# One bank of PSUM for every use, and new lists for four engines, in a vision transformer block on one core

## The chip, the core and the metric

One core of a Trainium2 chip runs the whole program. Its engines are TensorE (PE), VectorE (DVE), ScalarE (ACT), GpSimd (POOL) and SyncE (SP, which issues the DMAs). The metric is the device time of one execution in microseconds, the median of several runs.

## What is computed

For each of 128 images: 196 patches of 16x16 in three colours go through the real part of a 2-D FFT, weights and a projection to 192 features; a class token and positions are added (197 tokens). Then attention with 12 heads of 16 features, and after it attention with 12 heads of 64 features, whose queries and keys are layer-normalised per head and whose heads are weighted by gates (two shared, the best 2 of 10 routed).

```python
h = _L0_tok_ref(x, ...)                       # FFT patches, projection, class token, positions
h = h + _L0_attn_ref(_layernorm(h), ...)      # softmax(q k / 4) v, 12 heads of 16, then Wo
h = h + _L0_ffn_ref(_layernorm(h), ...)       # q, k normalised per head; softmax(q k) v; gates; proj
```

## The kernel before

The weights are loaded and prepared once. Then the images run through a software pipeline: the kernel works on four images at once, each at another stage. The order is written out by hand, in `ORDER`: one list of steps for PE, DVE, ACT and POOL. An entry such as `3:qk1_0` says: step `qk1`, number 0, of image i + 3. Each engine runs its list once a pass (`run_phases`), 131 passes for i from -3 to 127; steps whose image doesn't exist are left out at both ends. The engines share only semaphores: a step waits for what its data need, and for room in its PSUM bank.

PSUM has 8 banks of 128 x 512 numbers. Each use of a bank is one step's result on PE: it waits until the bank's last reader is done (`room_for`), signals that it is full (`made`), and the last reader signals it free (`read_out`). The banks are given out in `bank_uses` from `BANKS`: each kind of step has a ring, taken in the order of PE's list. `qk1` and `s1` share banks 0 and 1; `tok`, `x1T`, `v1`, `ctx` and `wo` have bank 2; `rstd`, `s2`, `pT`, `o2` and `proj` share 3, 4 and 5; `x2T`, `gl`, `qk` and `v2` have bank 6 and `ms` bank 7.

The steps, by image, with lines of PE and of who reads the bank:

- `fold` (DVE, L895) adds two mirrored halves of the image; `tok` (PE) projects it; DVE adds positions (L901) and takes the moments; POOL takes the root (L454); `nx1` normalises on DVE (L886 to L890).
- `x1T` turns it (L538), copied by ACT (L722) and DVE (L911). `qk1_0` to `qk1_2` make queries and keys of four heads each in fp16 halves: two copies on ACT (L731, L732), the low part on DVE (L916). `v1` goes to ACT (L737).
- `s1_0`, `s1_2` ... `s1_10`: scores of two heads at a time, on two banks, in 32-row parts of the array. DVE takes the negated maximum (L921), ACT the exponential with its sum (L745, twice a head), which frees the bank. DVE divides into v (`ctx`, L929, L933), `ctx0` to `ctx2` on PE in 32-column parts, copied by ACT (L751); `wo` follows, added by DVE (L943) with the second moments.
- `nx2`, `x2T` (L726, L953), `gl` and `gate` (DVE, ACT L763), `qk0` to `qk5` (copied by ACT, L756), squares on POOL (L493), `ms0` to `ms2` sum them in 32-column parts, `var` (ACT L770 to L775, DVE L1003 to L1007) takes the root. `rstd0` to `rstd5` spread it (PE), applied by DVE (L1028); high parts on ACT (L780 `rstd`, L785 `kh`), low parts on DVE (L1012 `lo`, L1018 `kl`).
- `s2_0` ... `s2_10`: scores of two heads, 64-row parts; maximum on DVE (L1034), exponential on ACT (L792); `gr` on DVE (L1041, L1044) and `sc` on POOL (L489) weight them; `pT_0` to `pT_11` turn them (L684), copied by ACT (L798); `o2_0` to `o2_5` in 64-column parts (ACT L803); `v2_0` to `v2_3` (DVE L996); `proj` (DVE L1051), then the store.

All matmuls but the turns of `pT` and `x1T`, `x2T` have line L500, that of a helper. `lasts` picks, of several steps, the last on each bank, so that one wait a bank is made.

Of the kernel before, what the change touches and what calls it, by code (L numbers as in the profile page):

```python
# [176 lines left out]
def bank_uses():  # L177

    uses, in_bank, turn = {}, [[] for _ in range(8)], {}
    for ahead, name, n in steps_of("pe"):  # L180
# [966 lines left out]
```

## Time and profile before

| | |
|---|---|
| Time, median of 3 runs | 6208.34 us (6207.62 to 6211.28) |
| The profiled execution | 6208.79 us, span 6207.0 us |
| PE busy | 5808.5 us, 94% |
| DVE busy | 5098.7 us, 82% |
| ACT busy | 4936.7 us, 80% |
| POOL busy | 2435.5 us, 39% |
| DMA | 17 GB/s over the span |

Busy time counts an engine while at least one instruction is in it; the ends of matmuls are modelled. The page cuts the span in 40 equal slices; the windows and the timeline show any stretch, in us from the span's start. In the timeline like instructions in a row are merged to one row.

### The profile page before, as it was taken

How to read it: one execution, taken by the hardware profiler on the slowest of the kernel's cores; microseconds unless marked ns; L12 is line 12 of the kernel's file. 1: busy time of each engine (PE TensorE's matmuls, PEld its weight loads, DVE VectorE, ACT ScalarE, POOL GpSimd, SP SyncE). 2: the span in 40 equal slices, each digit the busy share in tenths (PEclk: the TensorE clock that was granted, in tenths of full speed). 3: DMA queues.
4: the chain of work that ended last, by engine and by line, in shares of the span. 5: the costliest groups of instructions: out<-in, count | busy, mean ns of one | idle time of the engine just before them, and what ended most of it. 6: DMA issues, size and time to landing. Idle time of an engine off the chain costs nothing.

```text
span 6207.0 us, 204792 instructions
## 1 busy us (share of the span) xinstructions
PE 5808.5 (94%) x63792; PEld 4640.1 (75%) x63792; DVE 5098.7 (82%) x16573; ACT 4936.7 (80%) x18945; POOL 2435.5 (39%) x2438
## 2 busy tenths in 40 slices
PE   3899999999999999999999999999999999999998
PEld 3677777777777777777777777777777777777776
DVE  4788888888888888888888888888888888888886
ACT  1788887887888888788888878888887887888886
POOL 0333443343344344334334433433433343444343
PEclk8999999999999999999999999999999999999999
DMA  1000000000000000000000000000000000000000
GB/s 64 16 19 16 15 19 16 15 15 19 16 15 19 16 15 15 19 16 15 19 16 15 17 17 16 15 19 16 15 19 16 15 15 19 16 15 19 16 15 5
DMA packets 60493, 106.58 MB, mean 17 GB/s; under 512 B 8077, under 2 KB 33945, under 8 KB 60129
## 3 DMA queue, kind: packets, MB, share of 16 engines
q1 hardware_dynamic: 60456, 106.12, 5.6%
q8 instruction: 21, 0.34, 0.0%
q14 instruction: 16, 0.12, 0.0%
HBM read 86.72 MB, written 19.37 MB: 17 GB/s over the span
## 4 chain that ended last, share of the span: by engine, by line
PE 60%; DVE 27%; issue 8%; ACT 4%; DVEq 1%; SPq 0%; ACTq 0%; POOL 0%; DMA 0%; POOLq 0%
PE bank L500 54%; PE bank L684 6%; DVE nmax L1034 5%; DVE qkn L1028 4%; DVE qk L916 3%; ACT p L745 3%; DVE kl L1018 2%; DVE ql L1012 2%; DVE v L996 2%; DVE nmax L921 2%; DVE gn L1044 1%; DVE x1T L911 1%; DVE rsum L1041 1%; DVE rsum L929 0%; DVE glog L963 0%
## 5 line engine op out<-in xcount | busy, mean ns | idle before, releaser
L489 POOL TENSOR_TENSOR pq<-pq,gn 99x788 f32<-99x788 f32 x768 | 1166.3, 1519 | 2302.6 <-DVE gn L1044 2302.4
L792 ACT ACTIVATE pq<-bank,nmax 99x197 f32<-99x197 f32 x3072 | 1303.1, 444 | 300.5 <-DVE nmax L1034 300.5
L745 ACT ACTIVATE p<-bank,nmax 99x197 f32<-99x197 f32 x3072 | 1281.9, 441 | 31.2 <-DVE nmax L921 15.1
L921 DVE TENSOR_REDUCE nmax<-bank 99x2 f32<-99x394 f32 x1536 | 824.4, 565 | 320.8 <-PE bank L500 316.8
L1034 DVE TENSOR_REDUCE nmax<-bank 99x2 f32<-99x394 f32 x1536 | 837.9, 559 | 125.3 <-PE bank L500 110.1
L798 ACT ACTIVATE pT<-bank 99x394 f32<-99x394 f32 x1536 | 773.1, 512 | 152.7 <-PE bank L684 152.3
L684 PE MATMUL bank<-ident,pq 99*99 99x99 f32 (+1 forms) x6144 | 784.7, 260 | 14.8 <-ACT pq L792 3.3
L500 PE MATMUL bank<-x2T,wqkc 128*128 128x198 f16 (+1 forms) x7680 | 796.3, 249 | 1.0 <-ACT qkc L756 0.6
L684 PEld LDWEIGHTS bank<-ident,pq 99*99 99x99 f32 (+1 forms) x6144 | 647.5, 166 | 171.1 <-issue 78.4
L500 PEld LDWEIGHTS bank<-x2T,wqkc 128*128 128x128 f16 (+1 forms) x7680 | 650.0, 98 | 99.1 <-ACT qkc L756 41.4
L792 ACT ACTIVATION_READ_ACCUMULATOR pq<-bank,nmax 99x1 f32 x3072 | 687.9, 224 | 0.0
L745 ACT ACTIVATION_READ_ACCUMULATOR p<-bank,nmax 99x1 f32 x3072 | 677.0, 220 | 0.0
L493 POOL TENSOR_TENSOR sq<-qkc 128x396 f32<-128x396 f32 x768 | 660.2, 866 | 31.4 <-ACT qkc L756 24.7
L500 PE MATMUL bank<-pT,v 128*64 128x197 f32 x6144 | 633.7, 341 | 0.2 <-ACT pq L792 0.2
L780 ACT ACTIVATE qh<-qkn,ln_b 128x198 f16<-128x198 f32 x768 | 361.2, 470 | 334.2 <-DVE qkn L1028 334.1
L1028 DVE SCALAR_TENSOR_TENSOR qkn<-bank,ln_w,qkc 128x198 f32<-128x198 f32 x1536 | 575.7, 416 | 10.5 <-PE bank L500 5.0
L500 PE MATMUL bank<-qk 32*99 32x197 f16 x6144 | 418.8, 254 | 173.0 <-DVE qk L916 127.3
L500 PE MATMUL bank<-wp,oT 128*99 128x192 f32 x3072 | 530.6, 329 | 0.5 <-ACT oT L803 0.5
L500 PE MATMUL bank<-wv,x2T 128*99 128x384 f16 (+1 forms) x2560 | 518.2, 333 | 1.4 <-DVE v L996 1.4
L500 PEld LDWEIGHTS bank<-qk 32*99 32x99 f16 x6144 | 264.7, 120 | 336.6 <-issue 122.7
L500 PEld LDWEIGHTS bank<-wp,oT 128*99 128x99 f32 x3072 | 489.7, 166 | 18.3 <-ACT oT L803 1.1
L500 PEld LDWEIGHTS bank<-pT,v 128*64 128x64 f32 x6144 | 391.7, 137 | 129.6 <-issue 42.4
(149 smaller groups left out, 11877.8 us busy)
## 6 DMA issues: line engine op xcount, KB each, us to landing
xa<-in_xa SPq DMA_DIRECT2D x128, 300.1 KB
xb<-in_xb SPq DMA_DIRECT2D x128, 300.1 KB
out_tokens<-res SPq DMA_DIRECT2D x128, 74.2 KB
out_tokens<-res SPq DMA_DIRECT2D x128, 73.5 KB
p<-in_wq SPq DMA_DIRECT2D x1, 1152.0 KB
pT<-in_wk SPq DMA_DIRECT2D x1, 1152.0 KB
qkc<-in_basis SPq DMA_DIRECT2D x1, 661.5 KB
sq<-in_wq SPq DMA_DIRECT2D x1, 576.0 KB
```

The source lines that it names most:

```text
L489: nc.gpsimd.tensor_tensor(pair, pair, factor, op=ALU.mult).then_inc(s_sc.up(), 1)
L493: nc.gpsimd.tensor_tensor(sq[:, t], qkc[:, t], qkc[:, t], op=ALU.mult).then_inc(s_sq.up(), 1)
L500: return nc.tensor.matmul(o, l, r, start=first, stop=last)
L684: last = nc.tensor.transpose(o[0:TC, k * T + c * TC:k * T + c * TC + n], pq[0:n, h % SLOTS, c, k * TC:k * TC + TC], ident[0:n, 0:n])
L745: last = nc.scalar.activation(p1[0:TC, h, c, :], psum("s1", h)[0:TC, c * T:c * T + T], ACT.Exp, bias=nmax1[:, c, h:h + 1], accum_out=sum1[ ...
L780: nc.scalar.activation(qh[:, t, :], qkn[:, t % QKN_SLOTS, 0, :], ACT.Identity, bias=ln_b[:, 0:1]).then_inc(s_hi.up(), 1)
L792: last = nc.scalar.activation(pq[0:TC, h % SLOTS, c, 0:T], psum("s2", h)[0:TC, c * T:c * T + T], ACT.Exp, bias=nmax2[:, h, c:c + 1], accum ...
L798: nc.scalar.activation(pT[0:TC, h].rearrange("p a b -> p (a b)"), psum("pT", h)[0:TC, 0:2 * T], ACT.Copy).then_inc(free("pT", h), 1)
L916: V.scalar_tensor_tensor(qk1[:, g, 1].rearrange("p a b -> p (a b)"), psum("qk1", g)[:, 0:2 * TP], E1 ** -0.25 / W_SCALE, qk1[:, g, 0].rear ...
L921: V.tensor_reduce(nmax1[:, :, h], psum("s1", h)[0:TC, 0:2 * T].rearrange("p (a b) -> p a b", a=2), op=ALU.max, axis=AX.X, negate=True).the ...
L1028: last = V.scalar_tensor_tensor(qkn[:, t % QKN_SLOTS, s, :], psum("rstd", t)[:, s * TP:s * TP + TP], ln_w[:, s:s + 1], qkc[:, t, s, :], AL ...
L1034: V.tensor_reduce(nmax2[:, h, :], psum("s2", h)[0:TC, 0:2 * T].rearrange("p (a b) -> p a b", a=2), op=ALU.max, axis=AX.X, negate=True).the ...
```

## The change

The rings are gone. In PE's list each entry names its bank after an @, two digits where a step has two results: `3:s1_0@51` puts head 0 in bank 5 and head 1 in bank 1. The lists of all four engines are ordered anew. `LEAD` = 2 writes out two passes more at each end of the loop as straight code, and the count that a wait is for is worked out in another form for it. `lasts` is gone: a step that needs several banks read waits for the last of them. `ms` is numbered 0 in place of 2. The edits that repeat the ones below (o2, gr and DVE's ctx as PE's ctx; var as ms) are left out.

```diff
@@ -127,33 +127,30 @@
 
 
 
-BANKS = {"tok": (2,), "x1T": (2,), "qk1": (0, 1), "v1": (2,), "s1": (0, 1), "ctx": (2,), "wo": (2,),
-         "x2T": (6,), "gl": (6,), "qk": (6,), "v2": (6,), "ms": (7,),
-         "rstd": (3, 4, 5), "s2": (3, 4, 5), "pT": (3, 4, 5), "o2": (3, 4, 5), "proj": (3, 4, 5)}
-
 ORDER = {
     "pe": """
-3:tok 0:pT_9 0:pT_10 0:o2_3 0:pT_11 1:rstd1 0:o2_4 0:o2_5 1:s2_0 0:proj 1:v2_1 3:x1T 1:rstd2 1:s2_2 1:v2_2 1:rstd3
-3:qk1_0 1:v2_3 3:v1 3:s1_0 2:x2T 1:rstd4 1:s2_4 3:qk1_1 2:qk0 1:rstd5 1:pT_0 3:s1_2 2:gl 1:s2_6 1:pT_1 3:qk1_2 2:qk1
-1:pT_2 3:s1_4 3:ctx0 2:qk2 1:pT_3 1:s2_8 2:qk3 3:s1_6 2:ms0 2:qk4 1:o2_0 1:o2_1 3:s1_8 1:pT_4 1:pT_5 2:qk5 2:ms1
-3:s1_10 3:ctx1 1:s2_10 1:o2_2 2:ms2 2:v2_0 3:ctx2 1:pT_6 3:wo 1:pT_7 1:pT_8 2:rstd0
+3:tok@6 0:pT_7@2 1:v2_0@5 0:pT_8@1 1:rstd2@4 0:pT_9@2 0:pT_10@0 0:pT_11@6 0:o2_3@7 0:o2_4@3 0:o2_5@7 1:s2_0@03
+1:s2_2@64 1:rstd3@7 3:x1T@1 0:proj@2 1:rstd4@1 3:qk1_0@7 3:qk1_1@0 1:s2_4@36 3:s1_0@51 3:qk1_2@4 1:v2_1@2 3:s1_2@73
+1:v2_2@0 1:pT_0@1 1:v2_3@5 2:x2T@7 3:s1_4@14 3:v1@2 1:pT_1@3 1:s2_6@76 2:gl@1 2:qk0@3 2:qk1@0 1:rstd5@4 1:pT_2@2
+1:pT_3@1 3:s1_6@57 2:qk2@4 2:qk3@1 3:s1_8@03 3:s1_10@52 2:qk4@6 2:qk5@1 3:ctx0@7 1:s2_8@43 1:o2_0@0 1:pT_4@5 3:ctx1@6
+2:ms0@1 2:ms1 1:o2_1@2 2:ms2 3:ctx2@4 1:s2_10@03 1:pT_5@7 3:wo@6 1:o2_2@5 2:rstd0@1 1:pT_6@7 2:rstd1@4
 """,
     "dve": """
-3:fold 1:v2_0 1:var2 0:gr5 2:wo 1:rstd0 1:gate3 3:tok 1:kl0 1:rstd1 1:lo0 2:nx2 1:s2_0 3:nx1 1:lo1 1:s2_1 0:proj 1:kl1
-1:v2_1 1:rstd2 3:x1T 1:s2_2 1:lo2 1:v2_2 1:rstd3 1:s2_3 3:qk1_0 1:v2_3 1:kl2 3:s1_0 1:lo3 1:gr0 3:s1_1 2:x2T 1:s2_4
-1:s2_5 1:rstd4 1:gr1 1:kl3 3:qk1_1 1:rstd5 3:s1_2 3:s1_3 2:gl 1:s2_6 1:kl4 3:ctx0 1:lo4 1:s2_7 1:gr2 3:qk1_2 3:s1_4
-1:gr3 3:s1_5 1:lo5 1:s2_8 1:s2_9 3:s1_6 3:s1_7 1:kl5 3:ctx1 3:s1_8 3:s1_9 1:gr4 2:gate1 3:s1_10 3:s1_11 2:gate2
-1:s2_10 3:ctx2 1:s2_11
+3:fold 0:gr4 0:s2_10 0:s2_11 1:var2 2:wo 1:rstd0 1:rstd1 0:gr5 1:kl0 3:tok 1:v2_0 1:rstd2 1:lo0 1:kl1 1:lo1 3:nx1
+1:s2_0 1:s2_1 1:lo2 1:rstd3 1:s2_2 1:gate3 3:x1T 1:kl2 1:s2_3 2:nx2 1:rstd4 0:proj 3:qk1_0 1:s2_4 3:s1_0 1:gr0 3:qk1_1
+3:s1_1 1:v2_1 3:s1_2 3:s1_3 3:qk1_2 1:s2_5 1:kl3 1:lo3 1:gr1 3:s1_4 2:x2T 1:v2_2 3:s1_5 1:s2_6 1:kl4 1:s2_7 1:gr2 2:gl
+1:v2_3 1:rstd5 3:s1_6 3:s1_7 3:ctx0 1:gr3 1:lo4 3:s1_8 3:s1_9 3:s1_10 3:s1_11 3:ctx1 1:s2_8 1:s2_9 1:kl5 2:gate1
+2:gate2 3:ctx2 1:lo5
 """,
     "act": """
-3:x1T 1:rstd2 1:kh2 1:s2_2 3:qk1_0 1:rstd3 1:kh3 1:s2_3 3:v1 2:x2T 3:s1_0 3:s1_1 1:s2_4 3:qk1_1 1:s2_5 2:qk0 1:kh4
-1:pT_0 3:s1_2 3:s1_3 1:rstd4 1:s2_6 3:qk1_2 2:qk1 1:pT_1 1:s2_7 1:rstd5 3:s1_4 1:pT_2 2:qk2 1:pT_3 3:s1_5 1:kh5 2:qk3
-1:s2_8 3:s1_6 3:s1_7 1:s2_9 1:o2_0 2:qk4 3:s1_8 2:gate0 3:s1_9 1:o2_1 3:ctx0 1:pT_4 2:qk5 1:pT_5 3:s1_10 3:s1_11
-3:ctx1 1:s2_10 2:var0 3:ctx2 2:var1 1:s2_11 1:pT_6 1:o2_2 1:pT_7 2:rstd0 1:pT_8 2:kh0 1:pT_9 1:pT_10 1:o2_3 1:pT_11
-1:o2_4 1:o2_5 2:kh1 2:rstd1 2:s2_0 2:s2_1
+3:x1T 1:kh3 1:s2_2 1:rstd3 1:s2_3 3:qk1_0 1:kh4 1:rstd4 3:qk1_1 1:s2_4 3:s1_0 3:qk1_2 3:s1_1 3:s1_2 1:pT_0 3:s1_3
+2:x2T 1:s2_5 3:s1_4 1:pT_1 3:v1 3:s1_5 1:s2_6 2:qk0 2:qk1 1:pT_2 1:pT_3 1:s2_7 3:s1_6 3:s1_7 2:qk2 2:qk3 3:s1_8 3:s1_9
+3:s1_10 2:qk4 2:gate0 1:kh5 1:rstd5 2:qk5 3:s1_11 1:s2_8 1:o2_0 1:s2_9 3:ctx0 3:ctx1 3:ctx2 2:var0 2:var1 1:pT_4
+1:pT_5 1:s2_10 1:o2_1 1:s2_11 1:o2_2 2:kh0 2:rstd0 1:pT_6 2:rstd1 1:pT_7 2:kh1 1:pT_8 1:pT_9 1:pT_10 1:pT_11 1:o2_3
+2:rstd2 1:o2_4 2:kh2 1:o2_5 2:s2_0 2:s2_1
 """,
     "pool": """
-3:root1 1:h2c 2:h2b 1:sc0 1:sc1 1:sc2 2:sq0 3:h1b 2:sq1 2:sq2 1:sc3 2:sq3 1:sc4 2:sq4 2:sq5 1:sc5 3:root2
+3:root1 1:h2c 1:sc0 2:h2b 1:sc1 1:sc2 2:sq0 3:h1b 1:sc3 2:sq1 2:sq2 2:sq3 2:sq4 2:sq5 1:sc4 3:root2 1:sc5
 """,
 }
 
@@ -165,27 +162,23 @@
 def steps_of(engine):
 
     for entry in ORDER[engine].split():
-        ahead, step = entry.split(":")
+        ahead, step = entry.split("@")[0].split(":")
         name = step if step in WHOLE else step.split("_")[0] if "_" in step else step.rstrip("0123456789")
         number = step[len(name):].lstrip("_")
         yield int(ahead), name, int(number) if number else 0
 
 
 DEPTH = max(ahead for engine in ORDER for ahead, _, _ in steps_of(engine))
+LEAD = 2
 
 
 def bank_uses():
 
-    uses, in_bank, turn = {}, [[] for _ in range(8)], {}
-    for ahead, name, n in steps_of("pe"):
-        if name not in BANKS or (name == "ms" and n < 2):
-            continue
-        for i in (n, n + 1) if name in ("s1", "s2") else (n,):
-            ring = BANKS[name]
-            b = ring[turn.get(ring, 0) % len(ring)]
-            turn[ring] = turn.get(ring, 0) + 1
-            uses[name, i] = (b, ahead, len(in_bank[b]))
-            in_bank[b].append(ahead)
+    uses, in_bank = {}, [[] for _ in range(8)]
+    for entry, (ahead, name, n) in zip(ORDER["pe"].split(), steps_of("pe")):
+        for i, b in enumerate(entry.partition("@")[2]):
+            uses[name, n + i] = (int(b), ahead, len(in_bank[int(b)]))
+            in_bank[int(b)].append(ahead)
     return uses, in_bank
 
 
@@ -326,7 +319,8 @@
             shifts = [other - ahead + (p < place) for p, other in enumerate(in_bank[b])]
             if isinstance(img, int):
                 return sum(min(max(img + shift, 0), images) for shift in shifts)
-            return img * len(shifts) + sum(shifts)
+            whole = sum(shifts) // len(shifts)
+            return (img + whole) * len(shifts) + sum(shifts) - whole * len(shifts)
 
         def room_for(img, *key):
 
@@ -339,11 +333,6 @@
         def read_out(img, *key):
 
             return banks[uses[key][0]].free.sem, uses_before(img, key) + 1
-
-        def lasts(name, numbers):
-
-            last = {uses[name, n][0]: n for n in numbers}
-            return sorted(last.values())
 
         def full(*key):
             return banks[uses[key][0]].full.up()
@@ -404,11 +393,11 @@
                     if not edge or 0 <= i + ahead < images:
                         steps[name](i + ahead, n)
 
-            for i in range(-DEPTH, 1):
+            for i in range(-DEPTH, LEAD + 1):
                 go(i, True)
-            with eng.Fori(1, images - DEPTH) as i:
+            with eng.Fori(LEAD + 1, images - DEPTH - LEAD) as i:
                 go(i, False)
-            for i in range(images - DEPTH, images):
+            for i in range(images - DEPTH - LEAD, images):
                 go(i, True)
 
         @block.sync
@@ -591,8 +580,7 @@
                 o = psum("ctx", g)
                 pe.wait_ge(*room_for(img, "ctx", g))
                 pe.wait_ge(*s_vs.at(img, g + 1))
-                for h in lasts("s1", range(GROUP * g, GROUP * g + GROUP)):
-                    pe.wait_ge(*read_out(img, "s1", h))
+                pe.wait_ge(*read_out(img, "s1", GROUP * g + GROUP - 1))
                 for c in range(2):
                     for j in range(GROUP):
                         h = GROUP * g + j
...
@@ -691,8 +679,7 @@
                 pe.wait_ge(*room_for(img, "o2", t))
                 if t == 0:
                     pe.wait_ge(*read_out(img, "v2", 3))
-                for h in lasts("pT", (2 * t, 2 * t + 1)):
-                    pe.wait_ge(*read_out(img, "pT", h))
+                pe.wait_ge(*read_out(img, "pT", 2 * t + 1))
                 for c in range(2):
                     for j in range(2):
                         h = 2 * t + j
...
```

## Rows read from the trace of the kernel before

**Rows 1.** The page: span; busy time by engine; granted clock in 40 slices.

```profile
span 6207.0 us, 204792 instructions
...
PE 5808.5 (94%) x63792; PEld 4640.1 (75%) x63792; DVE 5098.7 (82%) x16573; ACT 4936.7 (80%) x18945; POOL 2435.5 (39%) x2438
...
PEclk8999999999999999999999999999999999999999
```

**Rows 2.** Windows, cut at starts of tok: length, then busy time by engine, clock, DMA.

```profile
80.47:223.80 143.33, 100.47 (x891) 75.54 (x892) 77.90 (x243) 68.34 (x270) 29.08 (x34) 0.77 0.05 14
3004.32:3051.46 47.14, 44.95 (x500) 35.97 (x499) 39.45 (x130) 38.53 (x149) 18.96 (x20) 1.00 0.05 16
6067.77:6114.90 47.13, 44.95 (x500) 35.95 (x498) 38.68 (x129) 38.54 (x149) 18.98 (x20) 1.00 0.01 3
6114.90:6207.00 92.10, 74.15 (x605) 55.15 (x603) 46.82 (x145) 50.58 (x175) 28.17 (x24) 0.85 0.02 6
```

**Rows 3.** Waits within one pass, of PE and of DVE: us in total, times, longest.

```profile
PE bank L500 <- DVE qk L916: 1.0, 2, 0.6
PE bank L500 <- ACT p L745: 0.9, 2, 0.6
...
DVE nmax L921 <- PE bank L500: 2.4, 4, 1.1
```

**Rows 4.** Timeline of PE in one pass: start, us, instructions [idle before <-releaser].

```profile
3016.97 0.29 PE L500 MATMUL bank<-kh,qh 64*99 64x197 f16 x2
...
3017.62 1.02 PE L500 MATMUL bank<-wv,x2T 128*99 128x384 f16 x5
...
3022.41 0.29 PE L500 MATMUL bank<-kh,qh 64*99 64x197 f16 x2
...
3023.72 1.04 PE L500 MATMUL bank<-x1T,wqk 128*128 128x198 f16 x10 [0.59 <-ACT p L745]
...
3025.72 0.56 PE L684 MATMUL bank<-ident,pq 99*99 99x99 f32 x4
3026.70 0.54 PE L500 MATMUL bank<-qk 32*99 32x197 f16 x8 [0.43 <-DVE qk L916]
...
3028.39 0.59 PE L684 MATMUL bank<-ident,pq 99*99 99x99 f32 x4
3028.83 1.04 PE L500 MATMUL bank<-x1T,wqk 128*128 128x198 f16 x10
...
3030.80 0.59 PE L684 MATMUL bank<-ident,pq 99*99 99x99 f32 x4
3031.95 0.54 PE L500 MATMUL bank<-qk 32*99 32x197 f16 x8 [0.56 <-DVE qk L916]
...
3036.77 0.54 PE L500 MATMUL bank<-sq,sel_var 128*32 128x198 f32 x8
3037.24 1.04 PE L500 MATMUL bank<-x2T,wqkc 128*128 128x198 f16 x10
...
3041.95 0.54 PE L500 MATMUL bank<-sq,sel_var 128*32 128x198 f32 x8
3042.78 0.54 PE L500 MATMUL bank<-qk 32*99 32x197 f16 x8 [0.29 <-ACT p L745]
```

**Rows 5.** The same timeline of PE: the two rows behind qk1_2 and qk4.

```profile
3029.71 1.03 PE L500 MATMUL bank<-x2T,wqkc 128*128 128x198 f16 x10
...
3038.21 1.56 PE L500 MATMUL bank<-pT,v 128*64 128x197 f32 x16
```

**Rows 6.** Timelines of DVE (first two) and ACT (last two) in the same pass.

```profile
3026.00 0.56 DVE L916 SCALAR_TENSOR_TENSOR qk<-bank,qk 128x396 f16<-128x396 f32 x1
...
3032.53 0.57 DVE L921 TENSOR_REDUCE nmax<-bank 99x2 f32<-99x394 f32 x1 [0.63 <-PE bank L500]
...
3037.60 0.43 ACT L745 ACTIVATE p<-bank,nmax 99x197 f32<-99x197 f32 x1
...
3038.40 0.44 ACT L745 ACTIVATE p<-bank,nmax 99x197 f32<-99x197 f32 x1
```

More of the change, by code:

```diff
@@ L621, in mean_square @@
                 if t == 0:
-                    pe.wait_ge(*room_for(img, "ms", 2))
+                    pe.wait_ge(*room_for(img, "ms", 0))
                 pe.wait_ge(*s_sq.at(img, 2 * t + 2))
@@ L625, in mean_square @@
                     q = 32 * (u % 4)
-                    last = mm(psum("ms", 2)[q:q + 32, 0:TP], sel_var[:, u, :], sq[:, u // 2, u % 2, :], t == 0, t == 2)
+                    last = mm(psum("ms", 0)[q:q + 32, 0:TP], sel_var[:, u, :], sq[:, u // 2, u % 2, :], t == 0, t == 2)
                 if t == 2:
-                    last.then_inc(full("ms", 2), 1)
+                    last.then_inc(full("ms", 0), 1)
             def qk(img, t):
@@ L767, in var_ @@
                 if n == 0:
-                    act.wait_ge(*made(img, "ms", 2))
+                    act.wait_ge(*made(img, "ms", 0))
                     act.wait_ge(*s_rs.at(img, 0))
-                    nc.scalar.activation(lnvar[:], psum("ms", 2)[:, 0:TP], ACT.Ln, bias=eps[:, 0:1]).then_inc(s_root.up(), 1)
+                    nc.scalar.activation(lnvar[:], psum("ms", 0)[:, 0:TP], ACT.Ln, bias=eps[:, 0:1]).then_inc(s_root.up(), 1)
                     act.wait_ge(*s_root.at(img, 1))
@@ L926, in ctx_ @@
                 hs = slice(GROUP * g, GROUP * g + GROUP)
-                for h in lasts("s1", range(GROUP * g, GROUP * g + GROUP)):
-                    dve.wait_ge(*read_out(img, "s1", h))
+                dve.wait_ge(*read_out(img, "s1", GROUP * g + GROUP - 1))
                 step(V.reciprocal(rsum1[:, :, hs], sum1[:, :, hs]), img, "ctx", g + 1)
@@ L1002, in var_ @@
                     dve.wait_ge(*s_root.at(img, 3))
-                    V.scalar_tensor_tensor(lnvar[:], psum("ms", 2)[:, 0:TP], LN_EPS, rootsq[:], ALU.add, ALU.mult).then_inc(free("ms", 2), 1)
-                    dve.wait_ge(*read_out(img, "ms", 2))
+                    V.scalar_tensor_tensor(lnvar[:], psum("ms", 0)[:, 0:TP], LN_EPS, rootsq[:], ALU.add, ALU.mult).then_inc(free("ms", 0), 1)
+                    dve.wait_ge(*read_out(img, "ms", 0))
                     step(V.scalar_tensor_tensor(rootsq[:], lnvar[:], -3.0, root[:], ALU.add, ALU.mult), img, "var", 1)
@@ L1038, in gate_over_sum @@
                 heads = slice(2 * t, 2 * t + 2)
-                for h in lasts("s2", (2 * t, 2 * t + 1)):
-                    dve.wait_ge(*read_out(img, "s2", h))
+                dve.wait_ge(*read_out(img, "s2", 2 * t + 1))
                 V.reciprocal(rsum2[:, heads, :], sum2[:, heads, :]).then_inc(s_rsum2.up(), 1)
@@ L1058, in build_vit_block @@
         for name, s in signals.items():
-            times = DEPTH + (3 if name in ("x_loaded", "stored") else 2)
+            times = DEPTH + (3 if name in ("x_loaded", "stored") else 2 + 2 * LEAD)
             assert s.made == times * s.per, (name, s.made, s.per)
```

## The prediction

> **What bounds the kernel now.** I read the page first: TensorE (PE) is busy 94% of the span, VectorE (DVE) 82%, ScalarE (ACT) 80%, GpSimd 39%, the DMA engines 6%, and the granted clock is 9 or more tenths in every slice but the first [rows 1]. The profiled execution took 6208.79 us for a span of 6207.0, so 1.8 us lie outside; that is 0.45 us over the median of the runs, and I set the forecast for the median equal to it.
>
> Then the table of windows, cut at the starts of `tok` [rows 2]. Three filling passes take 143.33 us, the last `tok` starts at 6067.77, and between 223.80 and 6067.77 lie 124 equal passes of 5843.97 / 124 = 47.13 us. So the question is one pass, 124 times. In it PE is busy 44.95 us, DVE 39.45, ACT 38.53, and the granted clock is 1.00: 2.19 us of the pass are idle on PE, 7.69 on DVE, 8.61 on ACT. PE is nearest to its limit, but not at it. The waits of this pass [rows 3] say what for: `s1` pairs for the low part of `qk1` (DVE), and matmuls for the exponentials (ACT `p`), which free banks 0 and 1.
>
> The timeline of PE shows the places [rows 4]. `s2_2` runs 0.65 us from its start to the next step's (3016.97 to 3017.62); `s2_4` takes 1.31 (3022.41 to 3023.72), because `qk1_1` behind it wants a bank that the exponentials of `s1` still hold: 0.66 lost. `pT_0` takes 0.98 (3025.72 to 3026.70) where `pT_1`, alone too, takes 0.44 (3028.39 to 3028.83): 0.54 lost to the DVE part of `qk1_1`. `pT_2` takes 1.15 (3030.80 to 3031.95): 0.6 to 0.7 lost to that of `qk1_2`. `ms1` takes 0.83 (3041.95 to 3042.78) where `ms0` takes 0.47 (3036.77 to 3037.24): 0.36 lost to an exponential. That is 2.2 us; read in the same way over all 62 steps, I count some 0.7 more in pieces of 0.04 to 0.20. So 2.2 (the idle time) to 2.9 us (from start to start) of the 47.13 are waits. Three of the four large ones are of one kind: `qk1` and the six `s1` pairs share two banks, so each `qk1` waits for the exponentials of the pair before, and then the next pair waits for ACT's and DVE's copies of it, with nothing between but what PE has in hand.
>
> **The change part by part.** The arithmetic of an image is the same: same matmuls, same reductions, same exponentials, same DMAs. What moves is the order and the bank.
>
> *Fewer switches of shape.* Between two matmul groups of full shape the start-to-start time is that of the streams: `qk1_2` to `qk1` 0.88 us (3028.83 to 3029.71). The same ten matmuls ahead of a group that uses a part of the array (`qk4` ahead of `o2_0`) take 0.97 (3037.24 to 3038.21) [rows 4, 5]. So a switch of shape costs 0.09 us. I count shapes in the two lists of PE: full (tok, wo, proj, pT, x1T, x2T, qk1, qk, v1, v2, gl, rstd), 32 rows (s1), 64 rows (s2), 64 columns (o2), 32 columns (ctx, ms). Before there are 35 switches in a pass, after 27 (`s2_0 s2_2`, `s1_8 s1_10`, `ctx1 ms0 ms1`, `o2_3 o2_4 o2_5` and the pairs of `qk` stand together). 8 x 0.09 = 0.72 us saved. Whether s2 and s1 side by side switch as well no row shows; I count them as a switch; the bound is 0 to 0.09 for two such places.
>
> *The floor of PE.* 47.13 - 2.9 - 0.72 = 43.5 us, or, if only the visible idle time can go, 47.13 - 2.19 - 0.72 = 44.2.
>
> *Do the old waits go?* Put PE's new list on a ruler at its unstalled lengths, with `tok` at 0: `proj` starts at 9.7, `qk1_0` 13.8, `qk1_1` 14.7, `s2_4` 15.7, `s1_0` 16.3, `qk1_2` 16.8, `s1_2` 18.6, `pT_0` 19.9, `s1_4` 21.7, `s2_6` 23.5, `s1_6` 27.5, `s1_8` 29.8, `s1_10` 30.2, `ctx0` 32.5, `s2_8` 33.3, `ctx2` 38.0, `s2_10` 38.8, `wo` 39.9, `rstd0` 42.75. Hand-overs come from rows [rows 6]: a DVE copy that starts at 3026.00 lets its matmul start at 3026.70 (0.70 later); a pair of `s1` that starts at 3031.95 lets its reduction start at 3032.53 (0.58); one head's exponentials take 0.80 on ACT (3037.60 to 3038.40). All three `qk1` now come together and each has a bank of its own (7, 0, 4), so no `qk1` waits for exponentials. `s1_0` needs DVE's part of `qk1_0`: 13.8, plus 0.8 of inner stream and 0.3 to land, ACT's two copies to 15.6, DVE's to 16.2, matmul at 16.35, against 16.30 on the ruler: 0.05 late. The next pairs need parts that are ready two microseconds before.
>
> *New waits on banks.* The tightest, by the same laying out of DVE's list (a reduction 0.48, `rstd` 0.67, a low part 0.33, `nx` 1.6, `tok` and `wo` 2.0) and ACT's (0.80 a head, 0.38 a `pT`): `pT_0` at 19.9 wants bank 1 from the exponentials of `s1_1`, done at 19.96 if DVE is on time, +0.1; `gl` at 24.1 wants bank 1 from `s1_4` at 24.05; `qk5` at 31.5 wants bank 1 from `qk3` at 31.45; `s2_8` at 33.3 wants bank 3 from `s1_9` at 33.0; `s1_4` wants bank 1 from `pT_0`, 0.4 to spare. The norm chains have room: `lo0` is done 1.6 before `s2_0`, the sequence `var0` to `var2` 0.6 before `rstd0`. Named new waits: some 0.15 to 0.2 us a pass. My lists on the ruler leave out the small hiccups of a real DVE (39.2 us by my lengths, against 39.45 busy and more with gaps), and there are five places within 0.1 us; I add 0.3. Below zero these waits can't be, so the bounds of this term are 0 and, from the rival below, 2.5; I take 0.5. POOL is passed over: `h2c` waits there for `proj`'s copy with `sc0` behind it, 15.5 + 0.9 = 16.4, and `sc0` waits longer for `gr0` (17.7), then takes 1.5, ready at 19.25, `pT_0` starts at 19.9.
>
> *The merged waits* (`lasts` gone): 3 + 6 waits less on PE and on DVE. ACT takes these steps in order, so the last one covers the others; they are waits for something that has happened. Ten matmuls with two met waits ahead of them take 0.88 us, 0.088 each [rows 4, 5], so a met wait can cost only a small part of one: I take 0, bounds 0 and -0.3 a pass.
>
> *Edges.* LEAD = 2 writes four passes more out as straight code. The last written-out full pass of before, 6067.77 to 6114.90, took 47.13 like the looped ones [rows 2], so 0. The filling passes run images one at a time, and there the ring of two banks costs most; the drain of 92.10 us gets the passes' rate partly. I take 8 us off the 235 of both; bounds 0 and 20.
>
> *Sum.* Pass 43.5 + 0.5 = 44.0. 124 x (47.13 - 44.0) = 388 us, edges 8: 6209 - 396 = 5813, say 5815 us.
>
> **The rivals.**
>
> *A, VectorE sets the pace.* DVE needs its 39.45 busy us and the gaps between, and every one of 24 score heads is a chain PE, DVE, ACT, PE. In the new order DVE must wait in places by the ruler: for `s2_8` 1.2 us, for `s2_10` 0.7, for `wo`, `tok` and `s2_4` 0.1 to 0.4 each, so some 3 us; 39.45 + 1.3 of gaps + 3 = 43.8, almost PE's own 44.0. If it is late at `proj` by d, then `s1_0`, `s1_1` and `pT_0` are late by nearly d. For it: four slacks within 0.1 us. Against it: the large waits of DVE stand where it has nothing to do. Price 0.8 to 2.5 us a pass: 5912 to 6123 us. The Trainium skill, page TensorEngine Tiling (Array Packing), section PSUM Bottleneck, says that packing speeds up TensorE but not the copying out, which may become the limit; by it this rival would hold, and its advice to use both ScalarE and VectorE is what the kernel does already.
>
> *B, no gain.* The free banks bring nothing, because the reads and not the count of banks end the waits: the 2.2 to 2.9 us come back in other places, and the switches saved are too little to see. Then at most 47.13 - 0.1: 6190 to 6220. Against it: the 0.66 at `qk1_1` is a wait for a bank and for nothing else.
>
> *C, slower.* One mechanism, at one place: DVE's stretch from `nx2` over `rstd4`, `proj`, `qk1_0`, `s2_4`, `s1_0`, `gr0` to `s1_1`, with ACT's exponentials behind, stands ahead of `pT_0` on PE, in order. If DVE gets to it late, all of PE's list stops. It decides once DVE is more than 3.7 us late there on each pass (43.5 + 3.7 = 47.2); at 4.5 us the time is 6209 + 124 x 0.9 = 6320.
>
> *D, the clock.* In the filling and draining windows the granted clock is 0.77 and 0.85, with waits of microseconds between matmuls; in the steady pass it is 1.00 with single waits of 0.66 [rows 2, 4]. If the new order had gaps long enough for the lower level (1.2 GHz) a tenth of the pass's work at half speed would add 4.4 us, a pass of 48.4, and 6209 + 124 x 1.3 = 6370. All gaps that I foresee are shorter than the present ones. The Trainium skill, page TensorE: Matmul & The Clock Gate, section A second HAM failure mode: psum-queue depth-cycling, says that cycling through banks makes short idles that throw the clock back; the pass of before cycles through all eight banks and shows 1.00, against it.
>
> **How the numbers follow.** Forecast 0.65 (pass 43.5 to 44.8, 5756 to 5912 us); A 0.24; B 0.05; C 0.04; D 0.02. The predicted time is the forecast's, 5815. The range goes from the floor of PE, 5756, into A up to a pass of 45.7, 6030; outside are half of the upper part of A and B, C, D, near 2 in 10. A difference under 0.2% (12 us) can't be told from none: faster 0.89, same 0.05, slower 0.06.
>
> **What would show it.** Right: passes of 43.6 to 44.6 us between `tok` starts, PE over 98% busy, no PE wait over 0.3 us on ACT `p` ahead of `qk1`, the DVE wait ahead of `s1` gone or under 0.1, `qk` ahead of a part shape still 0.97. A shows as PE waits on `bank<-qk`, `pT` and `s2` steps of 0.2 to 0.6 us each, with DVE at 95% or more. B shows as a pass of 47 with waits in new places, C as one large wait ahead of `pT_0`, D as PEclk under 9 in the middle slices. The forecast is wrong if small lateness adds up around the ring of three engines, which the ruler can't show.

## The result, and the profile after

The changed kernel takes 5659.53 us (5655.20 to 5662.58), against 6207.98 (6203.64 to 6211.28) of the kernel before beside it: a ratio of 0.912, interval 0.910 to 0.913. The direction was forecast, the size was not: 548 us were won where 393 were forecast, and the time lies 97 us below the range's low end.

The page after, the lines that answer [rows 1]:

```profile
span 5656.6 us, 205438 instructions
...
PE 5526.3 (98%) x63792; PEld 4586.4 (81%) x63792; DVE 5191.6 (92%) x16573; ACT 4853.3 (86%) x18945; POOL 2387.8 (42%) x2438
...
PEclk8999999999999999999999999999999999999999
...
PE 63%; ACT 25%; issue 7%; DVE 3%; ACTq 1%; POOL 0%; SPq 0%; DMA 0%; POOLq 0%; DVEq 0%
```

The last line is the chain that ended last, by engine. Before, that line read:

```profile
PE 60%; DVE 27%; issue 8%; ACT 4%; DVEq 1%; SPq 0%; ACTq 0%; POOL 0%; DMA 0%; POOLq 0%
```

VectorE has nearly left it, and a quarter of it now runs over ScalarE. PE's busy time fell by 282 us although it has the same 63792 matmuls, in a full pass from 44.95 to 42.84 us. Some 0.8 of these 2.1 us are the switches that the forecast had counted, and some 0.5 are short waits that busy time covers (the pass of before had 2.19 us of idle time and 3.2 us of waits). The other 0.8 are steps that take less time than before, and the first sign of what the forecast missed.

The windows after, cut at starts of `tok` as [rows 2] (length, then busy time of PE, PEld, DVE, ACT, POOL, the clock, DMA):

```profile
80.61:197.95 117.34, 89.46 (x881) 70.27 (x882) 77.02 (x244) 66.06 (x268) 27.29 (x33) 0.81 0.06 17
2992.55:3035.55 43.00, 42.84 (x500) 35.60 (x499) 40.24 (x129) 37.88 (x148) 18.59 (x19) 1.00 0.06 18
5529.38:5656.60 127.22, 109.43 (x1113) 88.31 (x1111) 85.25 (x272) 88.66 (x324) 47.18 (x43) 0.95 0.02 6
5486.50:5529.38 42.88, 42.66 (x500) 35.58 (x499) 39.90 (x130) 37.87 (x148) 18.56 (x19) 1.00 0.02 5
```

The three filling passes lost 26.0 us (143.33 to 117.34), the 124 full passes 512.5 (5843.97 to 5529.38 - 197.95 = 5331.43), and the time from the last `tok` to the end 12.0 (139.2 to 127.2): 550.5 together, the difference of the spans. A looped pass takes 43.00 us in place of 47.13; the last row is a full pass that is written out as straight code, and it takes 42.88 (42.86 from one start of `tok` to the next). That difference is a second sign of something unforeseen.

The timeline of PE in the looped pass, for the places of [rows 4 and 5]:

```profile
2994.97 0.51 PE L672 MATMUL bank<-ident,pq 99*99 99x99 f32 x4
2995.33 0.98 PE L489 MATMUL bank<-wv,x2T 128*99 128x384 f16 x5
...
3008.38 0.54 PE L489 MATMUL bank<-qk 32*99 32x197 f16 x8
3008.86 1.04 PE L489 MATMUL bank<-x1T,wqk 128*128 128x198 f16 x10
...
3011.12 1.02 PE L489 MATMUL bank<-wv,x2T 128*99 128x384 f16 x5
3012.15 0.59 PE L672 MATMUL bank<-ident,pq 99*99 99x99 f32 x4
3012.58 0.98 PE L489 MATMUL bank<-wv,x2T 128*99 128x384 f16 x5
...
3021.78 0.57 PE L489 MATMUL bank<-qk 32*99 32x197 f16 x16
3022.28 2.15 PE L489 MATMUL bank<-x2T,wqkc 128*128 128x198 f16 x20
3024.36 0.88 PE L489 MATMUL bank<-p,vs 128*32 128x197 f32 x16
```

No row is left with idle time before an `s1` pair (`bank<-qk`); [rows 4] had three. `s1_0` takes 0.48 (3008.38 to 3008.86), as always. But `s1_8` and `s1_10`, 16 matmuls, take 0.50 together (3021.78 to 3022.28): two pairs for little more than the price of one. `v2_2` ahead of `pT_0` takes 1.03 (3011.12 to 3012.15) against 0.86 for the same step in [rows 4] (3017.62 to the next step): a wait of 0.17. `qk4` and `qk5` take 2.08 (3022.28 to 3024.36) where twice 0.88 and a switch are 1.85: 0.23. Read through in the same way, 0.6 us of waits are left in a pass. A single `pT` takes 0.36 where PE comes to it without a stop (`pT_7`, 2994.97 to 2995.33) and 0.43 where it has waited for its bank (`pT_0`, 3012.15 to 3012.58, behind `v2_2`, a full shape too).

### The profile page after: what moved, and what is told of

Same layout as the page of the kernel before. It is cut to its first block, busy times and chain, and to the rows that moved or that the text cites. A ratio compares the mean times of both kernels' runs of the same rounds, so it can differ in the third digit from the quotient of the medians.

```text
span 5656.6 us, 205438 instructions
## 1 busy us (share of the span) xinstructions
PE 5526.3 (98%) x63792; PEld 4586.4 (81%) x63792; DVE 5191.6 (92%) x16573; ACT 4853.3 (86%) x18945; POOL 2387.8 (42%) x2438
## 4 chain that ended last, share of the span: by engine, by line
PE 63%; ACT 25%; issue 7%; DVE 3%; ACTq 1%; POOL 0%; SPq 0%; DMA 0%; POOLq 0%; DVEq 0%
PE bank L489 55%; ACT p L732 13%; PE bank L672 7%; ACT pq L779 6%; ACT qkc L743 4%; DVE nmax L1020 1%; ACT pT L785 1%; ACT qk L719 1%; PE bank L527 1%; SPq L406 0%; ACTq L730 0%; ACT v L724 0%; ACTq L729 0%; ACT x2T L713 0%; ACT qk L718 0%
## 5 line engine op out<-in xcount | busy, mean ns | idle before, releaser
L779 ACT ACTIVATE pq<-bank,nmax 99x197 f32<-99x197 f32 x3072 | 1338.8, 469 | 170.5 <-DVE nmax L1020 170.5
L732 ACT ACTIVATE p<-bank,nmax 99x197 f32<-99x197 f32 x3072 | 1317.0, 482 | 4.9 <-DVE nmax L908 4.9
L732 ACT ACTIVATION_READ_ACCUMULATOR p<-bank,nmax 99x1 f32 x3072 | 816.4, 266 | 0.0
L779 ACT ACTIVATION_READ_ACCUMULATOR pq<-bank,nmax 99x1 f32 x3072 | 772.5, 251 | 0.0
L785 ACT ACTIVATE pT<-bank 99x394 f32<-99x394 f32 x1536 | 716.1, 502 | 63.5 <-PE bank L672 48.6
L489 PE MATMUL bank<-x2T,wqkc 128*128 128x198 f16 (+1 forms) x7680 | 754.9, 249 | 8.4 <-DVE qkn L1014 0.2
L672 PE MATMUL bank<-ident,pq 99*99 99x99 f32 (+1 forms) x6144 | 754.8, 254 | 7.2 <-POOL pq L478 2.5
L471 POOL TENSOR_TENSOR h2c<-h2b,ones 99x384 f32<-99x384 f32 x128 | 105.9, 827 | 1235.9 <-DVE res L1036 1235.9
L772 ACT ACTIVATE kh<-qkn,ln_b 128x198 f16<-128x198 f32 x768 | 368.5, 480 | 222.0 <-DVE qkn L1014 222.0
L443 POOL TENSOR_TENSOR rstd<-vare,mhalf 99x2 f32<-99x2 f32 x256 | 178.2, 696 | 610.0 <-DVE vare L867 610.0
```

The lines of the kernel that those rows point to most:

```text
L489: return nc.tensor.matmul(o, l, r, start=first, stop=last)
L672: last = nc.tensor.transpose(o[0:TC, k * T + c * TC:k * T + c * TC + n], pq[0:n, h % SLOTS, c, k * TC:k * TC + TC], ident[0:n, 0:n])
L732: last = nc.scalar.activation(p1[0:TC, h, c, :], psum("s1", h)[0:TC, c * T:c * T + T], ACT.Exp, bias=nmax1[:, c, h:h + 1], accum_out=sum1[ ...
L772: nc.scalar.activation(kh[:, t, :], qkn[:, t % QKN_SLOTS, 1, :], ACT.Identity, bias=ln_b[:, 1:2]).then_inc(s_kh.up(), 1)
L779: last = nc.scalar.activation(pq[0:TC, h % SLOTS, c, 0:T], psum("s2", h)[0:TC, c * T:c * T + T], ACT.Exp, bias=nmax2[:, h, c:c + 1], accum ...
L785: nc.scalar.activation(pT[0:TC, h].rearrange("p a b -> p (a b)"), psum("pT", h)[0:TC, 0:2 * T], ACT.Copy).then_inc(free("pT", h), 1)
```

## Experiments

All are compared with the changed kernel's 5659.5 us and its pass of 43.00 us; runs of one group shared the runs of the kernel before, whose medians lay between 6206.4 and 6208.0. A pass is the time between two starts of `tok` in the middle of the trace.

### The banks alone

The new lists can't be run on the old rings: `s1_0` would want bank 1 from `qk1_1`, whose last reader stands behind `s1_0` in VectorE's new list. So the other half was run: old lists, free banks.

```diff
 ORDER = {   # the old lists; banks for PE's, each use on one that was read out before
-3:qk1_0 1:v2_3 3:v1 3:s1_0 2:x2T 1:rstd4 1:s2_4 3:qk1_1 2:qk0 ...
+3:qk1_0@6 1:v2_3@1 3:v1@7 3:s1_0@45 2:x2T@0 1:rstd4@6 1:s2_4@12 3:qk1_1@7 2:qk0@3 ...
```

> The four lists of the kernel before, in their old order, but every use has a bank of its own choice (for each, one that by the trace of before is read out at least 0.05 us before the use); merged waits and LEAD = 2 as in the changed kernel. Theory (the banks and the order work together: a part of the old waits is for banks, another part for data, and the order decides those): the 0.66 us before qk1_1 and the two or three bank waits behind ms1 and pT_3 go, the waits for the low part of qk1 (0.5 and 0.6) stay, so a pass of 45.8 to 46.3 us, and the three filling passes shorten by 5 to 25 us: 6050 to 6120 us. Rival 1 (the banks were all of it): pass 43 to 44.2, 5660 to 5820 us. Rival 2 (the banks alone bring nothing, since the lists' order holds every engine to the same waits): 6190 to 6215 us.

Measured: 6100.57 us (6098.44 to 6101.70), ratio 0.983 (0.981 to 0.985), a pass of 46.37 and filling passes of 132.41 in place of 143.33. The waits on PE in the trace:

```profile
3018.21 0.29 PE L489 MATMUL bank<-kh,qh 64*99 64x197 f16 x2 [0.41 <-ACT pq L779]
3021.93 0.54 PE L489 MATMUL bank<-qk 32*99 32x197 f16 x8 [0.40 <-ACT pq L779]
3027.13 0.54 PE L489 MATMUL bank<-qk 32*99 32x197 f16 x8 [0.91 <-ACT p L732]
3033.68 0.54 PE L489 MATMUL bank<-qk 32*99 32x197 f16 x8 [0.29 <-ACT p L732]
```

The idle time before `qk1_1` is gone, as expected, and so is nearly all of the 0.5 ahead of `s1_2`, which I had expected to stay (`pT_0` takes 0.51 for 0.98). But others stand in their place, one of 0.91 us for a bank of my choice. So this choice is worth 107 us, of which 94 in the full passes (124 x 0.76) and 11 in the filling. The merged waits and `LEAD` = 2 are in it too. Free banks need the new order to bring their worth; a better choice for the old lists might bring more than mine, and wasn't tried.

### The two pairs side by side

```diff
-3:s1_8@03 3:s1_10@52 2:qk4@6 2:qk5@1
+3:s1_8@03 2:qk4@6 3:s1_10@52 2:qk5@1
```

> The changed kernel with one entry of PE's list moved: s1_10 behind qk4 in place of right behind s1_8, so that the two pairs of 32-row parts no longer stand side by side. Theory P (PE's own time sets the pass everywhere): each pair then takes 0.47 us in place of 0.21 and 0.29, and one switch of shape more costs 0.09, so +0.53 us a pass, +66 us, about 5725 us. Theory A (in the stretch from s2_4 to qk5 ScalarE sets the pace, and PE waits there anyway for 0.2 to 0.35 us behind it): the loss is met by waits that shrink, +0.15 to +0.3 us a pass, 5678 to 5697 us. Rival (the two pairs don't really run side by side, the trace only shows it): only the switch, +0.09 us or less, under 5671 us.

Measured: 5682.04 us (5680.61 to 5684.71), +22.5, a pass of 43.18. Theory A. PE's timeline of this kernel:

```profile
3034.27 0.54 PE L489 MATMUL bank<-qk 32*99 32x197 f16 x8
3034.75 1.04 PE L489 MATMUL bank<-x2T,wqkc 128*128 128x198 f16 x10
3035.72 0.54 PE L489 MATMUL bank<-qk 32*99 32x197 f16 x8
3036.19 1.04 PE L489 MATMUL bank<-x2T,wqkc 128*128 128x198 f16 x10
3037.16 0.88 PE L489 MATMUL bank<-p,vs 128*32 128x197 f32 x16
3037.97 0.29 PE L489 MATMUL bank<-kh,qh 64*99 64x197 f16 x2
```

Each pair now takes 0.48 and 0.47 us, 0.95 in place of 0.50; so side by side they do overlap, and that is 0.45 us of PE's time, one of the two switches in it. From `s1_8` to `ctx0` PE needs 2.89 us (3034.27 to 3037.16) in place of 2.58 (3021.78 to 3024.36), since the wait of 0.23 inside is gone, and `ctx0` to `s2_8` takes 0.81 (3037.16 to 3037.97) in place of 0.94. What is left of 0.45 and a switch of 0.09 is 0.18 us a pass.

### Who sets the pace: one more instruction on ScalarE

The chain of the changed kernel within a pass goes over ScalarE from the maxima of `s2_4` to the copy of `qk3`, some 15 us; here its ends (start, us, what):

```profile
3001.88 6.50 PE bank L489 x57
3008.41 0.58 DVE nmax L1020
...
3011.45 1.36 ACT p L732 x6
...
3016.70 1.01 ACT p L732 x4
3017.70 0.81 ACT pq L779 x4
3018.52 0.75 ACT qkc L743 x2
...
3022.39 0.95 ACT qkc L743 x2
3023.34 0.05 issue
3023.39 1.85 PE bank L489 x26
```

```diff
 def v1_(img, _):        # on ScalarE; the second kernel has the line in o2 for t == 2
     act.wait_ge(*made(img, "v1", 0))
     nc.scalar.activation(v1[:]...).then_inc(free("v1", 0), 1)
+    nc.scalar.activation(spare[:, 0:D], wp2[:, 0, :], ACT.Copy)
```

> The changed kernel with one more instruction on ScalarE in each pass, a copy of 128x192 numbers to a tile of its own that nobody reads, right behind v1, in the stretch from s2_4 to qk3 where the chain of the trace runs over ScalarE. By the rows of qh (about 0.36 us from start to start) it takes 0.36 us there. Theory A (ScalarE sets the pace in this stretch): the pass grows by all of it, +0.33 to +0.4 us, +41 to +50 us, about 5703 us. Rival (PE sets the pace and ScalarE has slack): +0 to +0.1 us a pass, 5656 to 5672 us.

> The changed kernel with the same extra instruction on ScalarE, once a pass, but right behind o2_2, where ScalarE waits for VectorE next (kh0). Theory A (only the stretch from s2_4 to qk3 is bound by ScalarE, the rest of the pass by PE): nothing, 5655 to 5665 us. Rival (the whole ring is tight, any load on ScalarE delays it): +0.2 us a pass or more, over 5684 us.

Measured: inside the stretch 5695.13 us (5693.62 to 5697.10), +35.6, a pass of 43.28; outside it 5660.96 (5658.80 to 5664.49), +1.4, a pass of 43.03. The instruction itself took 0.45 and 0.41 us:

```profile
L727 ACT ACTIVATE spare<-wp 128x192 f32<-128x192 f32 x128 | 57.5, 449 | 0.0
...
L793 ACT ACTIVATE spare<-wp 128x192 f32<-128x192 f32 x128 | 52.5, 410 | 0.0
```

So the same load costs 0.28 us a pass in one place and 0.03 in the other. The trace of the first shows where it comes out: `s1_8` and `s1_10`, which want banks that ScalarE reads out, take 0.74 together in place of 0.50. ScalarE sets the pace in those 15 us, though it is busy for only 86% of the span. Outside them one place of ScalarE was tried, where it had idle time; that PE sets the pace there is shown for one more place by the next run. A little less than the estimated 0.36 came through.

### A switch of shape

```diff
-1:s2_0@03 1:s2_2@64 1:rstd3@7 3:x1T@1
+1:s2_0@03 1:rstd3@7 1:s2_2@64 3:x1T@1
```

> The changed kernel with rstd3 moved between s2_0 and s2_2 in PE's list: two switches of shape more in a pass, no other work. This place lies in the part of the pass where the chain runs over PE. Theory (a switch costs 0.09 us, and here it counts): +0.18 us a pass, +22 us, 5678 to 5688 us. Rival 1 (a switch costs time only where the first matmul behind it has to wait for its weights, or the gap is hidden): under 5668 us. Rival 2 (rstd3 waits for its bank, that of o2_5, read out late): +0.3 us or more, over 5695 us.

Measured: 5693.29 us (5688.64 to 5696.92), +33.8, a pass of 43.27: more than the theory's 0.18 us a pass, and just under what the second rival asked for. But there is no wait for the bank in it. In the tables of both traces the three steps take 1.57 us where they took 1.34: `s2_0` 0.65 for 0.55, `rstd3` 0.27 for 0.18, `s2_2` 0.65 for 0.61. The first two are the two switches, at 0.09 to 0.10. The third: side by side, the matmuls of `s2_2` take 0.43 from the first to the last, apart 0.47. That makes 0.23 of 0.27; the other 0.04 lies in pieces of 0.01, at `x1T`, now behind a part shape (0.36 for 0.35), and in the waits ahead of `s1_0`, `pT_0`, `qk5` and `s2_8`. A switch at a place where PE is on the chain costs its 0.09 to 0.10 us in full.

### Two banks renamed

```diff
-1:pT_0@1 1:v2_3@5 2:x2T@7 3:s1_4@14 3:v1@2 ... 2:qk5@1 3:ctx0@7 1:s2_8@43 ... 2:rstd0@1 ... 2:rstd1@4
+1:pT_0@2 1:v2_3@5 2:x2T@7 3:s1_4@24 3:v1@1 ... 2:qk5@4 3:ctx0@7 1:s2_8@23 ... 2:rstd0@4 ... 2:rstd1@2
```

> The changed kernel in the same order, with banks renamed from two places on to the end of the pass, for the two largest bank waits left: pT_0 takes bank 2 (read out by DVE's v2_1) and not bank 1 (exponentials of s1_1), and qk5 takes bank 4 (ACT's copy of qk2) and not bank 1 (ACT's copy of qk3, 0.4 us later). Theory A (ScalarE sets the pace of that stretch, through the banks that it frees): the 0.1 to 0.2 us ahead of pT_0 gain nothing, since the stretch is bound by ACT behind it, but qk5 starts 0.15 to 0.25 us earlier: pass 42.75 to 42.9, 5630 to 5648 us. Theory P (PE's own time, the bank waits simply add): both go, 0.3 to 0.4 us a pass, 5608 to 5622 us. Rival: the wait comes back at s2_8 (bank of s1_9): 5650 to 5665 us.

Measured: 5660.27 us (5658.49 to 5662.41), no difference. The third case: both waits are gone (`v2_2` 0.86 for 1.03, `qk4` 0.88 for 1.11), and came back at `pT_1` (0.74 for 0.44) and ahead of `s2_8` (`ctx0` 1.12 for 0.94). A bank wait removed inside a stretch that ScalarE paces only moves. The run shows one thing more: `pT_0` has the same step ahead of it as before, only the wait is gone, and now takes 0.35 in place of 0.43. Its written-out passes did shorten, though, from 42.86 to 42.74 us, and that led to the next runs.

### The loop itself

A looped pass works out on the engines' sequencers the counts that its waits compare with; a written-out one has them as constants. In the trace of the changed kernel a looped pass has 79 register steps on PE's sequencer, 74 on ScalarE's and 70 on VectorE's, a written-out pass none.

```diff
-LEAD = 2
+LEAD = 20
```

> The kernel with two banks renamed, and LEAD = 20 in place of 2: 36 passes more are written out as straight code, 84 are left in the loop. In the traces so far a written-out pass takes 42.86 us (changed kernel) or 42.74 (two banks renamed), a looped one 43.00 or 43.03, and the looped ones have register steps for the counts that they wait for, on ScalarE's sequencer 74 a pass. Theory (these steps lie on the chain through ScalarE): 36 x 0.29 = 10 us less, 5646 to 5653 us, and all written-out passes take 42.7 to 42.8 us. Rival (the first passes are shorter only because the pipeline is just filled): the added passes take 43.0 and the time stays at 5655 to 5664 us. Second rival (more code to fetch costs time): over 5665 us.

Measured: 5657.84 us (5655.92 to 5662.96). The total alone would speak for the rival; the windows don't. An early written-out pass, a looped one, and a late written-out one:

```profile
501.79:544.57 42.78, 42.50 (x500) 35.74 (x499) 39.78 (x130) 37.99 (x148) 18.54 (x19) 1.00 0.07 20
2651.76:2694.84 43.08, 42.57 (x501) 35.81 (x500) 39.99 (x131) 38.05 (x148) 18.59 (x19) 1.00 0.06 18
5018.79:5061.58 42.79, 42.50 (x500) 35.74 (x499) 39.78 (x130) 37.99 (x148) 18.55 (x19) 1.00 0.07 20
```

The late one is as short as the early one, so it isn't the freshly filled pipeline. The engines are almost equally busy (PE for 0.07 us more in the looped pass); most of the 0.29 us are idle time. In this trace, of the slowest of the four runs, the looped passes were 0.04 longer (43.07 against 43.03), the filling passes 3.9 us and the end 4.7 us longer than with LEAD = 2, which hid the gain. So the loop was written out nearly whole, with the renamed banks and with the kernel's own:

> The kernel with two banks renamed and LEAD = 60: 120 of the 131 passes are straight code, whose waits compare with constants. The run with LEAD = 20 had written-out passes of 42.79 us in its first and its last part, looped ones of 43.07. Theory (the register steps of the loop cost 0.14 to 0.29 us a pass and nothing takes their place): 120 passes at 42.8, 25 to 30 us less than with LEAD = 2, 5628 to 5642 us. Rival (instructions have to be fetched for every pass, and the fetches cost what the loop did): 5652 to 5670 us, or above.

> The changed kernel with its own banks and LEAD = 60. Its written-out passes took 42.86 us, the looped ones 43.00: 120 x 0.14 = 17 us less, 5638 to 5650 us; and 5 to 12 us over the one with two banks renamed, if those two bank waits count once the loop's steps are gone. Rival (the two are the same, as they were with LEAD = 2): within 4 us of each other.

Measured: 5637.78 us (5632.91 to 5640.42) with renamed banks, ratio 0.908 (0.907 to 0.910), and 5645.46 us (5642.75 to 5649.13) with the kernel's own. Both times lie in the ranges of their theories, though LEAD = 60 gave 22.5 us with renamed banks, where 25 to 30 were expected, and 14 in place of 17 with the kernel's own. The first of these is faster than both kernels, by 21.8 us against the changed one. Its page shows 8.45 MB of code on the first instruction queue, where the changed kernel had 0.61:

```profile
q8 instruction: 516, 8.45, 0.6%
...
PE 80%; ACT 14%; issue 3%; DVE 3%; SPq 0%; POOL 0%; DMA 0%; ACTq 0%; POOLq 0%; DVEq 0%
```

ScalarE's share of the chain says nothing here. With the same banks and LEAD = 2 it was 1%:

```profile
PE 95%; DVE 2%; issue 2%; ACT 1%; SPq 0%; POOL 0%; DMA 0%; POOLq 0%; DVEq 0%; ACTq 0%
```

and with the kernel's own banks it rose from 25 to 30% as the loop went. Two engines are so close to one another in this stretch that the chain falls now to one and now to the other.

Where the loop costs its time shows when a written-out and a looped pass of the changed kernel are laid side by side, step by step. Four places differ, all on PE: the looped pass takes 0.06 more at `o2_4` and `o2_5`, 0.08 more ahead of `s1_0` and 0.14 more ahead of `s2_8`, and it waits 0.14 less ahead of `pT_0`, whose bank ScalarE frees at the same time in both. So 0.28 are lost, and half of it only shortens a wait. The last place, in the written-out pass and in the looped one (`ctx0`, the exponential of `s1_9` that frees a bank for `s2_8`, and `s2_8`):

```profile
272.64 0.88 PE L489 MATMUL bank<-p,vs 128*32 128x197 f32 x16
272.94 0.30 ACT L732 ACTIVATION_READ_ACCUMULATOR p<-bank,nmax 99x1 f32 x1
273.45 0.29 PE L489 MATMUL bank<-kh,qh 64*99 64x197 f16 x2
...
3024.36 0.88 PE L489 MATMUL bank<-p,vs 128*32 128x197 f32 x16
3024.66 0.30 ACT L732 ACTIVATION_READ_ACCUMULATOR p<-bank,nmax 99x1 f32 x1
3025.30 0.29 PE L489 MATMUL bank<-kh,qh 64*99 64x197 f16 x2
```

ScalarE frees the bank 0.60 us behind the start of `ctx0` in both passes; `s2_8` starts 0.21 us later in one and 0.34 in the other. In between stand the waits of `s2_8` on PE's own sequencer, about 0.1 us apart; these are those of the looped pass:

```profile
L652 PEldq EVENT_SEMAPHORE  x1: 51/51/51, 3025.0 to 3025.0; - x1
...
L653 PEldq ALU_OP  x1: 32/32/32, 3025.1 to 3025.1; - x1
...
L654 PEldq EVENT_SEMAPHORE  x1: 51/51/51, 3025.2 to 3025.2; - x1
```

So ScalarE is no slower in the loop: it is PE's sequencer that has more steps left behind the wait that ends last. That its register steps are the cause, and not another difference of looped code, is argued from these places; they weren't taken away by themselves. The two bank waits that meant nothing in the loop are worth 7.7 us without it (passes of 42.78 against 42.89 us).

### The merged waits

```diff
-    pe.wait_ge(*read_out(img, "pT", 2 * t + 1))
+    for h in lasts("pT", (2 * t, 2 * t + 1)):
+        pe.wait_ge(*read_out(img, "pT", h))
```

(likewise for `ctx` on PE and DVE, and for `gr`.)

> The changed kernel with the waits merged by the change put back, one for each bank (PE: ctx and o2; DVE: ctx and gr). Theory: they are waits for what has happened, and cost nothing: 5650 to 5668 us. Rival: each costs its step on the sequencer, 0.03 to 0.1 us where nothing hides it: +0.3 to +1.5 us a pass, 5695 to 5840 us.

Measured: 5672.52 us (5671.88 to 5673.27), +13.0, a pass of 43.10: between the two. With the new banks this is 15 waits more on PE and 15 on VectorE, where the rings of before had needed 8 and 9. In the table of PE's steps nearly all of the 0.10 stands at one place, ahead of `o2_5` (`o2_4` 0.77 in place of 0.68); in the written-out passes it is 0.01. There PE waits for ScalarE to read out the bank of `o2_3`, and the wait put back is one step more behind that. A wait that has been met costs nothing where something hides it, and 0.09 us where it stands behind the one that ends last.

## Why the prediction failed

*What bounds the kernel*, the 124 equal passes and the nature of the large waits: right. `qk1` and `s1` wait for one another no more, and the idle rows before `bank<-qk` are gone.

*The waits that stay*: 0.5 us a pass forecast, 0.6 measured, all but 0.01 at places that the forecast had named as tight: `pT_0` (0.17, bank of `s1_1`), `qk5` (0.23, bank of `qk3`), `s2_8` (0.14, bank of `s1_9`) and `s1_0` (0.08). The last two are gone in the written-out passes, so the steps of the loop are in them, which the forecast had not reckoned with. That the sum came out so near is partly luck: 0.3 of the 0.5 was a lump for hiccups. No wait came at `gl`. So the rivals fall: A in its form (DVE's share of the chain is 3%, though it is busy for 92%), though another engine than PE does set the pace of a third of the pass, ScalarE, which the forecast named only as a link; B, C and D aren't seen (the clock is 1.00).

*The floor of PE*, 43.5 us: this is the step that failed. With 43.00 measured and 0.6 of waits in it, the floor is 42.4, 1.1 us lower. It was taken as the old pass less its waits and the switches, which holds each step's own length fixed, and the lengths moved. Added over all 62 steps, the time from a step's first matmul to its last fell by 0.8 us a pass:

- `s1_8` and `s1_10` side by side use different rows of the array and four banks, and overlap: from `s1_8` to `qk4` 0.50 us where the ruler had 0.85 (0.38 and 0.47). The prediction counted the pairs as neighbours and asked only whether a switch lay between. That is 0.33 us of the steps' own length (against the unpacked run, 0.45 with a switch).
- The 12 `pT` fell by 0.21 us in sum, the four `v2` by 0.08, `tok`, `wo` and `proj` by 0.16. They take longer where PE comes to them from a part shape or out of a wait: from first to last matmul `pT` 0.34 and not 0.26, `v2` 0.69 and not 0.65, `tok` 2.51 and not 2.44. That a wait alone does it shows in two runs where the step ahead is the same and only the wait is gone: `pT_0` in the run with two banks renamed (0.34 to 0.26), and `tok` in the run with the old lists (2.51 to 2.44). The price of a switch or of a wait is thus more than the gap ahead; I read [rows 5] for the gap before the next step and didn't look at that step's length.
- `s2_2` behind `s2_0` takes 0.04 less; smaller changes both ways make up the rest.

The other 0.3 us of the floor: the waits of the old pass were counted as 2.9 us, and the same reading, with each gap measured against the same hand-over elsewhere, gives 3.2; the 8 switches gave 0.8 in place of 0.72. So waits, switches and lengths fell by 2.5, 0.8 and 0.8 us, which is 4.1 of a pass (47.13 to 43.00); forecast were 2.4, 0.7 and nothing. The pass is 1.0 us shorter than 44.0, and 124 x 1.0 = 124 us of the 155 that the forecast was short; the edges are the other 30.

*The range's low end* was the floor itself, 5756 us (its own terms give 6209 - 124 x 3.62 - 8 = 5752). That is the second fault: a floor that rests on lengths under another order isn't a bound, and no case of mine lay below it.

*Edges*: 8 us forecast, 38 measured (26.0 in filling, 12.0 at the end), beyond the bounds of 0 and 20. The run with the old lists gives 11 of the 26 to the banks and leaves 15 to the order; the reason given was right, the size was a guess. The split is rough: in the runs with the extra instruction outside and with `rstd3` moved the filling took 122 us and the end 124 to 125, where the changed kernel has 117 and 127.

*The merged waits*: taken at 0 with bounds of 0 and -0.3; the run that put them back gives 0.1.

*LEAD and the loop*: taken at 0, because I took the pass of 6067.77 to 6114.90 [rows 2] for a written-out one. It isn't: it is pass 124, the last of the loop. The one full pass that the kernel before writes out comes right behind the filling, and it was shorter:

```profile
223.83:270.74 46.91, 44.63 (x501) 35.97 (x499) 39.31 (x130) 38.61 (x149) 18.89 (x20) 1.00 0.06 18
```

So a difference of 0.2 us stood in the trace already. In the changed kernel it is 0.14, in the run with the old lists a written-out pass was longer than a looped one (46.52 against 46.37). The cost to the forecast is small, since LEAD = 2 moves only four passes.

## What to carry to other kernels

A floor that is built from the lengths of steps must be rebuilt from their neighbours: what stands before a matmul group, a part shape or a wait, decides its length as well as the gap before it, and two groups on different rows and banks may share their time. Ask in which stretch each engine is on the chain, since the same 0.4 us of load cost 0.28 in one stretch of ScalarE and 0.03 outside it, and a bank wait taken away in the first only moved; an engine's share of the chain on the page doesn't settle it where two engines nearly tie. When an order is tuned until three engines are near their limit, waits already met and the steps of a loop begin to cost, where they stand behind the wait that ends last; they should be measured anew at the end.
